# Attention over edges: the exponentials go to two PSUM banks, and the experts' first-layer ring goes from four banks to two

## The reference

```python
h = (x_flat @ W_gat).reshape(M, HEADS, NUM_EXPERTS)          # 4 heads x 4 experts
e = leaky_relu(a_src[src] + a_dst[dst], 0.2)
e_max = segment_max(e, dst);  ee = exp(e - e_max[dst])
denom = segment_sum(ee, dst);  alpha = ee / (denom[dst] + 1e-16)
agg = segment_sum(h[src] * alpha[:, :, None], dst)           # -> layer norm, top 2 of 4 -> gates g
...
for ei in range(NUM_EXPERTS):
    hh = gelu(x @ W1[ei] + b1[ei])                           # 256 -> 512
    out = out + g[..., None] * (hh @ W2[ei] + b2[ei])        # 512 -> 256
```

## Time and profile before

| | us |
|---|---|
| median of three runs | 3457.8 (3450.46 to 3463.17) |
| the profiled execution | 3481.48 |
| its span, first to last instruction | 3479.7 |
| busy in the span: PE / POOL / DVE / ACT | 2048.6 / 1540.5 / 1332.3 / 880.3 |
| `gat_gather_experts` in the span | about 1635 to 3237 |

### The profile page before, as it was taken

The page is one execution under the profiler, slowest core; times in us unless marked ns, Lnnn a source line. Parts: engine busy times, 40 slices in busy tenths (PEclk is TensorE's granted clock), DMA queues, the critical chain, the costliest instruction groups (busy, mean ns, idle before and its releaser), DMA issues. The chain is left out here.

```text
span 3479.7 us, 27168 instructions
## 1 busy us (share of the span) xinstructions
PE 2048.6 (59%) x7626; PEld 1351.9 (39%) x7626; DVE 1332.3 (38%) x2595; ACT 880.3 (25%) x1886; POOL 1540.5 (44%) x1568
## 2 busy tenths in 40 slices
PE   5588777776776677446212110299159179996135
PEld 4444444443444444335101000166136156674033
DVE  6354344444454444466000000043024034545259
ACT  3324344333433343314000000033013013322110
POOL 2566565555555555521777777501721710000600
PEclk8789988887888888765555555599579589998555
DMA  5523223333333332437200100011001011111806
GB/s 160 201 85 88 81 86 105 99 118 92 118 104 115 92 120 84 154 110 246 75 10 10 19 9 9 7 53 61 10 25 61 10 41 51 43 59 48 233 2 231
DMA packets 197373, 288.96 MB, mean 83 GB/s; under 512 B 43736, under 2 KB 148023, under 8 KB 195830
## 3 DMA queue, kind: packets, MB, share of 16 engines
q0 software_dynamic: 63792, 121.66, 12.9%
q1 hardware_dynamic: 95030, 120.85, 10.6%
q10 hardware_dynamic: 38416, 44.96, 3.7%
HBM read 201.55 MB, written 85.80 MB: 83 GB/s over the span
## 5 line engine op out<-in xcount | busy, mean ns | idle before, releaser
L790 POOL DMA_INDIRECT ag_msg<-xn_tab,step_src x832 | 808.2, 971 | 594.3 <-PE ag_ps L1015 322.2
L1673 POOL DMA_INDIRECT edge_rows<-hx_d,gat_src x656 | 653.8, 997 | 507.6 <-DMA sums_d<-edge_rows 297.4
L1858 PE MATMUL ex_psY<-ex_w,ex_hh 128*128 128x256 f32 x1568 | 394.1, 412 | 510.7 <-issue 487.4
L1015 PE MATMUL ag_ps<-ag_msg,ag_hot 128*128 128x257 f32 x1664 | 492.0, 438 | 148.8 <-issue 92.5
L811 DVE TENSOR_TENSOR acc<-acc,ag_ps 128x257 f32 x832 | 351.8, 423 | 584.2 <-PE ag_ps L1015 190.0
L1785 DVE TENSOR_TENSOR hi_one_low<-hi_numbers,hi_low 128x2048 bf16<-128x2048 f32 x64 | 146.3, 2286 | 1086.9 <-remote 685.5
L1858 PEld LDWEIGHTS ex_psY<-ex_w,ex_hh 128*128 128x128 f32 x1568 | 319.5, 207 | 583.0 <-issue 506.8
L1846 PE MATMUL ex_psF<-ex_yT,ex_w 128*128 128x448 f32 x896 | 369.4, 567 | 144.7 <-issue 112.3
L1015 PEld LDWEIGHTS ag_ps<-ag_msg,ag_hot 128*128 128x128 f32 x1664 | 334.3, 215 | 293.7 <-issue 146.2
L1903 ACT COPY ex_yo<-ex_psY 128x256 f32<-128x256 f32 x196 | 73.0, 372 | 915.1 <-remote 600.0
L1192 ACT ACTIVATE gat_self<-iota_row,step_nloc 128x128 f32<-128x128 f32 x832 | 257.0, 388 | 173.2 <-PE ag_ps L1015 110.6
(11 more groups left out here) (365 smaller groups left out, 2164.3 us busy)
## 6 DMA issues: line engine op xcount, KB each, us to landing
y_d<-ex_yo ACTq DMA_DIRECT2D x28, 896.0 KB
co_rows<-y_d SPq DMA_DIRECT2D x28, 896.0 KB
ag_msg<-xn_tab,step_src POOLq DMA_INDIRECT x832
xnT<-base_d SPq DMA_DIRECT2D x7, 1792.0 KB
edge_rows<-hx_d,gat_src POOLq DMA_INDIRECT x656
base_d<-xnT ACTq DMA_DIRECT2D x7, 1024.0 KB
sums_d<-edge_rows SPq DMA_DIRECT2D x5, 1344.0 KB, 4.6
xg<-in_x_dram SPq DMA_DIRECT2D x7, 896.0 KB, 5.7
```

What stands on the lines that cost most here:

```text
L790: pool.indirect_dma_start(msg[:, q, u, 0:D], None, c.xn_tab, bass.IndirectOffsetOnAxis(ap=t.idx[:, at:at + 1], axis=0)).then_inc(s_g[q], 16)
L1015: nc.tensor.matmul(bank[u % BANKS][:, 0:ROWW], hot[:, k, u, :], msg[:, k, u, :], start=True, stop=True).then_inc(s_mm, 1)
L1673: pool.indirect_dma_start(G[:, j % RING, w, :], None, c.hx_d, bass.IndirectOffsetOnAxis(ap=plan.idx[:, at + w:at + w + 1], axis=0)).then_i ...
L1858: last = nc.tensor.matmul(bank[:, 0:D], hh[:, k].rearrange("p a b -> p (a b)")[:, u * P:(u + 1) * P], w2[:, e, k, :], start=(k == 0), stop ...
```

## The change

`ex` moves from SBUF to PSUM: a tensor of 1024 values per partition (two banks), of which the two halves (the factors that rescale the old sums, and the weights) take 448 each, one bank per half. To make room, `FB` goes from 4 to 2. All else is as it was; on every engine the instructions and their order are the same, and only addresses, the shape of the write of line 1916 (2 x 448 instead of 896 in one row) and the counts in the waits on `s_ge` differ. The line numbers behind line 1575 grow by one.

```diff
@@ gat_gather_experts
-    FB, YB = 4, 2
+    FB, YB = 2, 2
...
-        ex = sb("gs_ex", [P, 2, HEADS, BLOCK])
+        ex = ps("gs_ex", [P, 1024])[:].rearrange("p (i n) -> p i n", i=2)[:, :, 0:HEADS * BLOCK].rearrange(
+            "p i (h w) -> p i h w", h=HEADS)
```

## The result

The kernel before ran at a median of 3460.5 us (3450.5 to 3464.7, six executions), the changed one at 3481.8 us (3478.6 to 3488.9, six). The ratio, estimated over the executions, is 1.0079, 95% interval 1.0049 to 1.0109: 17 to 38 us slower. (The quotient of the two medians, 1.0062, lies inside it.) The forecast was 3483 (3464 to 3498).

What follows compares the result with a forecast made beforehand. The stage was taken as nearly the gathers' time plus PE's full-pace work when they rest. Terms 15.0 + 11.5 + 1.5 - 3 gave +25 us on 3457.8, so 3483 us, range 3464 to 3498.

Steps and rivals of the forecast that it cites:

- steady ring of two: First-layer units in ordinary running: 0.23 us of slack with two banks is enough, so 0 us.
- stall in five due turns: Turns 7, 12, 17, 22, 27, while ACT is away: two units more behind the stall, 3.0 us each, 15.0 us.
- slow clock behind them: PE after the due turns' gap, grown from 1.5 to 4.5 us: clock halves, 2.3 us each, 11.5 in all.
- after the first gather stretch: When ACT comes back at 2264.44, unit 2 waits for Gelu 0, about one unit later: +1.5 us (0 to 3).
- swallowed by gather stretches: Second and third gather stretches take back a quarter of the 12.1 us lost before them: -3 us (0 to -12.1).
- `ex` in PSUM: DVE's multiply and scans and ACT's writes of `ex`: no extra cost from PSUM, 0 us.
- The stage as a sum: Whole stage: nearly the gathers' time plus PE's remaining full-pace work, so PE's losses outside gather stretches count whole.
- The clock holds: Rival, due turns: PE keeps full clock after the longer gap, so only +14.5 us, 3472 us; chance 0.14.
- The restart: PE and ACT resuming after the first gather stretch: unit 2 about one unit later, +1.5 us (0 to 3).
- The ring stalls in every unit: Rival, some 25 full-pace turns: each of 6 units pays 0.1 to 0.3 us, +30 on top, 3513 us; chance 0.10.
- The gathers swallow all before them: Rival, second and third gather stretches: all losses before them vanish, leaving +16 us, 3474 us; chance 0.08.
- Faster: Rival, first gather stretch: ACT's instructions come sooner, one turn and a half gained, -13 us, 3445 us; chance 0.09.

Runs made afterwards that it cites:

- two_undue: Kernel before with four banks, but PE waits as with two banks in all turns except 2, 7, 12, 17, 22, 27; ratio 0.9988 to the kernel before.
- fill: Kernel before with two banks, `ex` in SBUF, and five idle matmuls on PE behind unit 1 in the five due turns; ratio 1.0046 to the kernel before.
- after: The changed kernel itself, `ex` in PSUM and two banks, against the kernel before; ratio 1.0079, stage 1624.1 us.
- fb2_only: Kernel before with only the ring cut to two banks, `ex` staying in SBUF; ratio 1.0083 to the kernel before.
- rep_before: The kernel before run once more, unchanged; ratio 1.0000 to the kernel before, stage 1595.5 us.
- two_late: Kernel before with four banks, but PE waits as with two banks in turns 17, 22 and 27 alone; ratio 1.0057 to the kernel before.
- two_early: Kernel before with four banks, but PE waits as with two banks in turns 7 and 12 alone; ratio 1.0010 to the kernel before.
- hist2_after: Changed kernel with two histogram batches per set moved behind unit 1 of each due turn, the others one layer earlier; ratio 1.0052 to the kernel before.

## Why the prediction was right, and which terms were off

| step | forecast, us | measured, us |
|---|---|---|
| steady ring of two | 0 | 0: two_undue 0.9988, ordinary turns unchanged |
| stall in five due turns | 3.0 each, 15.0 | 3.0 each (fill: 29.88 - 26.87) |
| slow clock behind them | 2.3 each, 11.5 | 1.5 to 3.1 each; 12.2 in all after, 11.6 in fb2_only |
| after the first gather stretch | 1.5 (0 to 3) | turn 2 +2.8 against before's trace; its store 4.7 later than in rep_before |
| swallowed by gather stretches | -3 (0 to -12.1) | -5.9 after against before; 4 to 5 over all traces |
| `ex` in PSUM | 0 | no loss; about -0.4 at the stage's end |
| sum | +25 | +23.1 in the profiled stage, +21 in the medians |

The measured column adds up: 27.2 in the due turns, 2.8 in turn 2, less 5.9, less 0.5 before turn 2 and 0.5 behind turn 27, is 23.1.

- **The number.** That 3481.8 came within 2 us of 3483 is partly luck: the median of before is now 3460.5, where the forecast started from 3457.8. The difference is the fair test, +25 against +21 to +23.
- **The stage as a sum** held: two_late's loss arrives whole, two_early's in part.
- **The clock** was the disputed step. "The clock holds" fell in after and in fb2_only, ten due turns of ten, and fill shows the sum it would have given (stage +12.7 against before's trace, for a forecast of 14.5). The size 2.3 came from a choice between 1.5 and 2.5, and is right as a mean only; one turn pays 1.5, another 3.1. Two of its precedents were read from the wrong rows: the 4.86 and 2.98 us of the earlier trace rows are idle times of the weight loads, and PE itself stood 4.19 and 2.57 us there. The 4.05 and 5.27 us of the earlier trace rows, on which the step can rest alone, are PE's own.
- **The restart** was mis-sized: "comes about one unit later, 1.5 us" left out that PE comes out of the gather stretch at half clock and with two banks gets to full clock only behind the restart, and it took the one trace's lead of three units for the rule. rep_before, two_late and two_early have four ready. With the clock it is 2.8 against that trace and 4.7 against those.
- **What the gathers swallow** was taken at a quarter of 12.1; it is nearer to 5 than to 3. The two misses, one upward and one downward, cancel in the sum.
- **The ring stalls in every unit** fell (two_undue). **The gathers swallow all before them** fell: at turn 14 the changed kernel was still 7.1 us late. **Faster** fell: turn 1's store is 0.5 us earlier, no turn and a half. (Its sum is 25 - 38 = -13, not 38 - 25.)
- **`ex` in PSUM.** A scan by itself goes from 491 to 496 ns and a multiply from 2025 to 2021, but the scans overlap and follow each other faster: the 20 of the sixth span take 7.17 us where all twelve traces with `ex` in SBUF have 7.42 or 7.43. The estimate of 1.4 us by the Trainium skill's fixed cost ("VectorE: DVE Perf Modes", section "The TRN2 errata — SBUF-src ops pay a fixed extra latency per instruction"), 65 ns on each, is not in these rows. ACT's write is 1.08 us instead of 1.02 in a due turn, and 3.82 instead of 3.93 for the four at the end. So the end of the stage is some 0.4 us shorter: from the last turn's store to the stage's end it is 47.3 and 47.5 us in the two kernels with `ex` in PSUM (after, hist2_after), in the others 47.6 to 48.1.

## What to carry to other kernels

When a ring gets shorter, look not at its steady run but at the places where its consumer goes away for a while: there each bank fewer puts one more unit behind the stall, and a gap that was short enough for PE's clock may not be any longer. If such a gap can't be avoided, other PE work put into it buys back the clock, even idle work, so long as that work was not already filling a stall elsewhere. Read a gap from the rows of the engine that you mean: the weight loads had stood 2.98 us where PE had stood 2.57. Read small effects from the length of a repeated piece (here one turn, repeatable to 0.02 us) and not from a whole that differs by 5 us between executions.

## What the runs showed of the hardware that I had not expected

- Between the gaps that always and never cost the clock lie some that do either. In the due turns PE's clock held after 0.75 us (fill, five of five) and 1.5 us (25 of 25 in six traces), after 2.25 us in three of five, and after 3.00, 3.12 and 4.5 us in none of 25. Where it fell, the turn lost 1.4 to 3.1 us, not always the same for one gap.
- The prices bunch: 1.4 to 1.8 us in nineteen turns, 2.5 to 3.1 in eight. The granted clock tells them apart. In the nineteen it stood at 1.2 GHz for 3.4 us, and had fallen at most 0.5 us before PE went on, or up to 1.4 us after. In the eight it had fallen 0.6 to 1.7 us before PE went on, and stood there for 6.8 us. Turns 7 (3.1 us) and 12 (1.6 us) of the changed kernel, the stretches at half clock:

```profile
2379.80:2386.60 6.80, 6.00 (x8) 2.83 (x9) 6.73 (x16) 1.89 (x4) 0.00 (x0) 0.50 0.00 0
2646.10:2649.40 3.30, 3.04 (x4) 1.50 (x5) 2.87 (x8) 0.73 (x2) 0.00 (x0) 0.50 0.01 2
```

Half of PE's busy time in such a stretch is the price (3.0 and 1.5 us here). What sets the moment at which the clock falls stays open; no run here varied what stands ahead of the gap.
- Two executions of one program differ by 5.5 us in this stage, all of it up to the store of turn 14, where the gathers run. What in the gathers sets it was not tried.
